# Gated delta attention with a mixture of experts: unnormalised queries, one joint sum of squares, reordered engine lists

## The reference, cut to what matters

```
q = silu(short_conv(hn @ Wq));  k = silu(short_conv(hn @ Wk));  v = silu(short_conv(hn @ Wv))
q = q * rsqrt(sum(q*q) + 1e-6) * 128 ** -0.5
k = k * rsqrt(sum(k*k) + 1e-6)
S = S * exp(g);  S = S + k (beta * (v - k.S))^T;  o = q.S            # one step per token
y = o * silu(gate);  y = y * rsqrt(mean(y*y) + 1e-5) * norm_w;  out = y @ Wo
```

## Time and profile before

| what | value |
|---|---|
| median of 3 runs | 5584.86 us (5580.64 to 5585.17) |
| the profiled execution | 5584.48 us, span 5582.7 us |
| busy over the span | PE 5247.8 us (94%), DVE 4446.0 (80%), ACT 3294.2 (59%), POOL 2364.0 (42%) |
| stretch 0 to 280 us (layer norm, decays) | PE 146.51 us, DVE 190.45, granted TensorE clock 0.79 |
| stretch 280 to 4730 us (the units) | PE 4297.46, DVE 4126.70, ACT 3113.79, POOL 2305.09, clock 1.00 |
| stretch 4730 to 5583 us (output projection and mixture) | PE 803.78, DVE 128.90, ACT 82.97, POOL 0.00, clock 0.97 |

### The profile page before, as it was taken

How to read it: one execution, slowest core, us unless ns; L and a number is a source line. 1 busy time by engine, 2 the same in 40 slices (tenths; PEclk the granted TensorE clock), 3 DMA queues, 4 the chain that set the end, 5 groups by cost and what they waited for, 6 DMA issues and landing times. The chain is left out here.

```text
span 5582.7 us, 88628 instructions
## 1 busy us (share of the span) xinstructions
PE 5247.8 (94%) x27460; PEld 3612.7 (65%) x27460; DVE 4446.0 (80%) x8285; ACT 3294.2 (59%) x6732; POOL 2364.0 (42%) x3687
## 2 busy tenths in 40 slices
PE   5599999999999999999999999999999998899999
PEld 2277777777777777777777777777777776344444
DVE  6699999999999999999999999999999997121110
ACT  3377767676767676767776767676767675010110
POOL 2155555555555555555555555555555553000000
PEclk8799999999999999999999999999999999899999
DMA  2111111111111111111111111111111110331121
GB/s 79 42 33 39 31 38 31 38 32 38 32 37 32 38 32 38 32 38 32 39 32 37 33 38 32 37 32 38 32 37 33 30 32 19 117 106 62 64 77 51
DMA packets 192055, 235.77 MB, mean 42 GB/s; under 512 B 41576, under 2 KB 136424, under 8 KB 187504
## 3 DMA queue, kind: packets, MB, share of 16 engines
q1 hardware_dynamic: 111016, 188.22, 11.5%
q10 hardware_dynamic: 80584, 41.95, 2.6%
HBM read 183.75 MB, written 46.38 MB: 41 GB/s over the span
## 5 line engine op out<-in xcount | busy, mean ns | idle before, releaser
L739 PE MATMUL bank<-xT,weights 128*128 128x512 f32 x4096 | 2090.9, 608 | 33.2 <-PEq L157 33.2
L1060 DVE SCALAR_TENSOR_TENSOR conv<-pre,taps,conv 128x512 f32<-128x512 f32 x1152 | 1006.4, 882 | 13.3 <-ACT conv L1284 8.1
L758 PE MATMUL bank<-KQ,KR 128*128 128x128 f32 x7168 | 984.5, 280 | 8.0 <-DVE KQ L1075 7.2
L758 PEld LDWEIGHTS bank<-KQ,KR 128*128 128x128 f32 x7168 | 895.9, 191 | 84.1 <-issue 61.5
L1075 DVE TENSOR_TENSOR KQ<-KQ,decay_u 128x512 f32<-128x512 f32 x896 | 868.9, 970 | 56.9 <-PE bank L758 40.3
L739 PEld LDWEIGHTS bank<-xT,weights 128*128 128x128 f32 x4096 | 675.6, 192 | 297.0 <-issue 286.0
L1507 POOL TENSOR_TENSOR KR<-KR,decay_u 128x256 f32<-128x256 f32 x768 | 579.9, 755 | 537.8 <-PE bank L758 537.1
L1090 DVE COPY_PREDICATED all_pairs<-level_mask,bank 128x512 f32<-128x512 int32 x896 | 794.1, 886 | 0.0
L1364 ACT ACTIVATE X<-bank 128x256 fp32r<-128x256 f32 x768 | 296.8, 386 | 601.4 <-PE bank L816 601.4
L1501 POOL TENSOR_TENSOR KR<-KR,decay_u 128x128 f32<-128x128 f32 x128 | 117.1, 915 | 1187.3 <-PE bank L758 1187.3
L790 PEld LDWEIGHTS bank<-T_inv,pairs 128*128 128x128 f32 x1536 | 275.5, 190 | 318.0 <-issue 303.2
(11 more groups left out here) (192 smaller groups left out, 9568.0 us busy)
## 6 DMA issues: line engine op xcount, KB each, us to landing
decay_u<-decay_scratch SPq DMA_DIRECT2D x128, 510.0 KB
beta_u<-beta_scratch SPq DMA_DIRECT2D x128, 256.0 KB
y_in<-y_scratch SPq DMA_DIRECT2D x32, 1024.0 KB, 4.8
y_scratch<-y_rn ACTq DMA_DIRECT2D x112, 256.0 KB, 2.3
xt<-in_L_attn_hidden_states SPq DMA_DIRECT2D x8, 1024.0 KB, 5.4
x_in<-in_L_attn_hidden_states SPq DMA_DIRECT2D x28, 256.0 KB, 5.1
out<-o_out ACTq DMA_DIRECT2D x28, 256.0 KB, 2.0
w<-in_L_ffn_W SPq DMA_DIRECT2D x8, 704.0 KB, 5.0
```

Of the source, the lines that this page charges most:

```text
L739: last = nc.tensor.matmul(bank[w % 2][:], weights[par][:, w, k, :], xT[:, k, u % J * UC:(u % J + 1) * UC], start=k == 0, stop=k == KC - 1)
L758: last = nc.tensor.matmul(to[:, :, i], KR[:, cols(i)], halves(KQ[:, :, cols(i)], l, 1), start=True, stop=True)
L1060: nc.vector.scalar_tensor_tensor(conv[:, w], taps_from(w, t), taps[par][:, w, t:t + 1], conv[:, w], ALU.mult, ALU.add).then_inc(steps.sem, 1)
```

## The change

1. The queries stay unnormalised. ScalarE writes SiLU of the convolved queries straight into KQ and squares them with a factor into `out_sq[a % 4]`; the query's norm, its square's rest on GpSimd, its sum on TensorE, Ln and Exp on ScalarE and the scaling on VectorE (L1195) are gone.
2. GpSimd adds the squares of the gated output to `out_sq` (`add_squares`), ScalarE rounds the total to float32r (`round_squares`), GpSimd takes what the rounding lost (`out_squares_left`), and TensorE sums both with a float32r matrix of 1/128 in place of the float32 product. The epsilon of the last root becomes 1e-5·1e-6·128.
3. KQ is doubled (`KQ[a % 2]`): the unit's inputs wait for `scan_ready` of unit b, not of m.
4. The halo of queries and keys is two copies of 16 elements.
5. The lists are reordered: level 0 ahead of one projection piece on TensorE; on VectorE the three query taps in a row at the start, the halo of queries and keys directly after the last identity, ahead of the first value tap and the scaling of level 5, and the residual ahead of the hats; on ScalarE the table load behind `take_delta`, and `round_squares` ahead of `take_right_side`; on GpSimd `first_x` behind the key scaling of level 4, followed by `add_squares`.
6. The last token's query goes the same way as the others: its own sum, norm and scaling are gone, and its squares are added to the last sum as a second matmul. The setup has one more memset and one more copy for the new constants.

Not shown in the diff are the declarations of the tiles and semaphores, and the renamed indices that follow from them.

```diff
-            def sums(which):
+            def key_sums():
 
                 if a is None:
                     return
-                wait(pe, squares_rest_ready, a, which + 1)
-                if which == 1:
-                    wait(pe, sums_taken, a, 1)
-                elif m is not None:
-                    wait(pe, sums_taken, m, 2)
+                wait(pe, squares_rest_ready, a, 1)
+                if m is not None:
+                    wait(pe, sums_taken, m, 1)
                     if c is not None and c >= 1:
                         pe.wait_ge(y_sums_free, c)
-                nc.tensor.matmul(bank[2][:], ones_r[:], squares[:, which, :], start=True, stop=False)
-                nc.tensor.matmul(bank[2][:], ones_r[:], squares_rest[:, which, :], start=False,
+                nc.tensor.matmul(bank[2][:], ones_r[:], squares[:], start=True, stop=False)
+                nc.tensor.matmul(bank[2][:], ones_r[:], squares_rest[:], start=False,
                                  stop=True).then_inc(sums_done.sem, 1)
...
-                    wait(pe, sums_taken, a, 2)
-                wait(pe, y_sq_ready, c, 1)
-                if m == LAST_UNIT:
-                    pe.wait_ge(tail_q_steps, 3)
-                nc.tensor.matmul(bank[2][:], mean_ones[:], y_sq[:], start=True, stop=True).then_inc(y_sums_done.sem, 1)
+                    wait(pe, sums_taken, a, 1)
+                wait(pe, out_sq_rest_ready, c, 1)
+                nc.tensor.matmul(bank[2][:], mean_r[:], out_sq_r[:], start=True, stop=False)
+                nc.tensor.matmul(bank[2][:], mean_r[:], out_sq_rest[:], start=False,
+                                 stop=True).then_inc(y_sums_done.sem, 1)
...
             project(2, (0, 1))
             inverse_z(1)
+            level(0)
             project(2, (2,))
-            level(0)
             inverse_t(1)
...
             first_delta()
-            sums(0)
             level(6)
             refine(b, 0)
-            sums(1)
-            if m == LAST_UNIT:
-                tail_sum()
+            key_sums()
             project(1, (0, 1))
             transpose_keys()
             y_sums()
...
-                if first:
-                    nc.vector.memset(pre[:, rows, :, 0:TAPS], 0.0).then_inc(ready.sem, 1)
-                else:
-                    nc.vector.tensor_copy(pre[:, rows, :, 0:TAPS], pre[:, rows, :, P:P + TAPS]).then_inc(ready.sem, 1)
+                for w in rows:
+                    if first:
+                        last = nc.vector.memset(pre[:, w, :, 0:TAPS], 0.0)
+                    else:
+                        last = nc.vector.tensor_copy(pre[:, w, :, 0:TAPS], pre[:, w, :, P:P + TAPS])
+                last.then_inc(ready.sem, 1)
...
-                wait(dve, rnorm_ready, a, 2)
-                nc.vector.tensor_tensor(k_hat, silu[:, 1], rnorm[:, 1], ALU.mult).then_inc(hats_ready.sem, 1)
+                wait(dve, rnorm_ready, a, 1)
+                nc.vector.tensor_tensor(k_hat[:], k_hat[:], rnorm[:], ALU.mult).then_inc(hats_ready.sem, 1)
...
-                if m is not None:
-                    wait(dve, scan_ready, m, 1)
-                decay = products(s.odd, 0)
-                nc.vector.scalar_tensor_tensor(KQ[:, 0], k_hat, -1.0, decay, ALU.mult, ALU.mult)
-                nc.vector.scalar_tensor_tensor(KQ[:, 1], silu[:, 0], SCALE, rnorm[:, 0], ALU.mult,
+                if b is not None:
+                    wait(dve, scan_ready, b, 1)
+                wait(dve, q_sq_ready, a, 1)
+                nc.vector.scalar_tensor_tensor(KQ[a % 2][:, 0], k_hat[:], -1.0, products(s.odd, 0), ALU.mult,
                                                ALU.mult).then_inc(unit_ready.sem, 1)
 
             place_last_query()
...
             place_last_query()
-            convolve(0, (1,))
-            halo(m, s.m_first, b, v_conv_steps, TAPS - 1, slice(2, 3), v_halo_ready)
+            convolve(0, (1, 2, 3))
+            halo(m, s.m_first, b, v_conv_steps, TAPS - 1, (2,), v_halo_ready)
             normalised_output()
             correct_delta(0)
             add_identity_to_z(1)
-            convolve(0, (2,))
             scale(0)
             keep_pairs(0)
             take_residual(c, 1)
...
             scale(2)
             keep_pairs(2)
             gated_output()
-            convolve(0, (3,))
             convolve(1, (1,))
             add_identity_to_z(4)
             scale(3)
...
             convolve(1, (2, 3))
             add_identity_to_z(5)
             scale(4)
-            convolve(2, (1,))
             keep_pairs(4)
             add_identity_to_z(6)
+            last_query()
+            halo(z, s.z_first, a, qk_conv_steps, 2 * (TAPS - 1), (0, 1), qk_halo_ready)
+            convolve(2, (1,))
+            scale(5)
             convolve(2, (2,))
-            scale(5)
-            last_query()
-            halo(z, s.z_first, a, qk_conv_steps, 2 * (TAPS - 1), slice(0, 2), qk_halo_ready)
             keep_pairs(5)
             convolve(2, (3,))
             scale(6)
             keep_pairs(6)
+            take_residual(b, 0)
             hats()
-            take_residual(b, 0)
             keep_chunk_decay()
-            if m == LAST_UNIT:
-                dve.wait_ge(tail_q_steps, 4)
-                nc.vector.scalar_tensor_tensor(tail_hat[:], tail_q[:], SCALE, tail_rnorm[:], ALU.mult,
-                                               ALU.mult).then_inc(tail_hat_ready, 1)
             unit_inputs()
...
-            def silu_squares(w):
+            def silu_queries():
                 if a is None:
                     return
-                wait(act, qk_conv_steps, a, (w + 1) * (TAPS - 1))
-                if w == 0 and m is not None:
+                wait(act, qk_conv_steps, a, TAPS - 1)
+                if b is not None:
+                    wait(act, scan_ready, b, 1)
+                nc.scalar.activation(KQ[a % 2][:, 1], conv[:, 0].rearrange("p b t -> p (b t)"),
+                                     ACT.Silu).then_inc(q_silu_ready.sem, 1)
+                wait(act, q_silu_ready, a, 1)
+                nc.scalar.activation(out_sq[a % 4][:], KQ[a % 2][:, 1], ACT.Square,
+                                     scale=LN_EPS ** 0.5 / SCALE ** 2).then_inc(q_sq_ready.sem, 1)
+
+            def silu_keys():
+                if a is None:
+                    return
+                wait(act, qk_conv_steps, a, 2 * (TAPS - 1))
+                if m is not None:
                     wait(act, unit_ready, m, 1)
-                nc.scalar.activation(silu[:, w], conv[:, w].rearrange("p b t -> p (b t)"),
+                nc.scalar.activation(k_hat[:], conv[:, 1].rearrange("p b t -> p (b t)"),
                                      ACT.Silu).then_inc(silu_ready.sem, 1)
-                wait(act, silu_ready, a, w + 1)
-                nc.scalar.activation(squares[:, w], silu[:, w], ACT.Square).then_inc(squares_ready.sem, 1)
+                wait(act, silu_ready, a, 1)
+                nc.scalar.activation(squares[:], k_hat[:], ACT.Square).then_inc(squares_ready.sem, 1)
...
+            def round_squares():
+                if c is None:
+                    return
+                wait(act, out_sq_added, c, 1)
+                nc.scalar.activation(out_sq_r[:], out_sq[c % 4][:], ACT.Copy).then_inc(out_sq_rounded.sem, 1)
...
-            silu_squares(0)
+            silu_queries()
             if m == LAST_UNIT:
                 tail_squares()
             take_x(4)
...
             square_output()
             keep_z(5)
             silu_gate()
-            silu_squares(1)
+            silu_keys()
             take_t(b, 5)
             take_x(5)
+            round_squares()
             take_right_side()
             take_x(6)
-            nc.scalar.preload_act_table_set("natural_log_exp_and_others")
             take_projection(0)
             take_delta()
-            inverse_norm(0)
+            nc.scalar.preload_act_table_set("natural_log_exp_and_others")
             first_tap(0)
-            inverse_norm(1)
-            if m == LAST_UNIT:
-                tail_inverse_norm()
+            inverse_norm()
             keep_scaled()
...
+        def add_squares(u):
+
+            if u is None:
+                return
+            wait_apart(pool, y_sq_ready.sem, y_sq_ready.at(u, 1), pool_waits_passed)
+            nc.gpsimd.tensor_tensor(out_sq[u % 4][:], out_sq[u % 4][:], y_sq[:], ALU.add).then_inc(out_sq_added.sem, 1)
+
+        def out_squares_left(u):
+
+            if u is None:
+                return
+            wait_apart(pool, out_sq_rounded.sem, out_sq_rounded.at(u, 1), pool_waits_passed)
+            nc.gpsimd.tensor_tensor(out_sq_rest[:], out_sq[u % 4][:], out_sq_r[:],
+                                    ALU.subtract).then_inc(out_sq_rest_ready.sem, 1)
 
...
-                squares_left(s.a, 0)
-                squares_left(s.a, 1)
+                squares_left(s.a)
                 for l in range(2, LEVELS - 1):
                     gather_x(s.b, l, None)
```

(29 more changed lines are left out.)

85 lines of the change are left out of this document (41 added, 44 removed).

## The result

The changed kernel takes 5452.14 us (5451.18 to 5453.22, 4 runs) against 5585.01 for the kernel before; the ratio is 0.9764, with a 95% interval of 0.9748 to 0.9779. So it is 133 us faster, where 183 were forecast; the time lies in the range of 5,345 to 5,510 us. It does not lie in the forecast's own band (5,340 to 5,430, chance 0.60) but in that of the tail rival (5,430 to 5,530, chance 0.27).

What follows compares the result with a forecast made beforehand. TensorE was taken as the bound, VectorE close behind. Per step 34.94 − 0.86 − 0.51 − 0.40 + 0.35 = 33.5 us, for the run −183 us to 5,401; own band 5,340 to 5,430 (0.60), range 5,345 to 5,510.

Steps and rivals of the forecast that it cites:

- tail rival: Step's end: ScalarE's T of level 0 late for the first inverse product, 0.70 us a step; 5,430 to 5,530 us, chance 0.27.
- TensorE's own work: Query sum gone (0.52 us) and output sum as two float32r matmuls (0.34 saved): 0.86 us a step, 110 us.
- The wait on delta: TensorE's level-pair product waits for ScalarE's delta; moving table load and halo copies gains 67 of 83.7 us, 0.13 a step stays.
- XX: TensorE's inverse product waits for GpSimd's XX, 0.40 us a step; moving the third query tap removes all 51 us.
- The pair of casts: GpSimd's small casts, 1.36 us beside two VectorE taps; one tap moved away saves 0.47 us.
- The new wait: Rounding on ScalarE waits for GpSimd's addition, delaying X for TensorE's first delta: 0.35 us a step, 45 us lost.
- slower rival: Between last identity and scaling of level 5, two halo copies each wait out a GpSimd instruction: 5,663 us, chance 0.07.
- level 6 on VectorE: Sign of the late step end: TensorE waits at level 6 on VectorE.
- T of level 0 late on ScalarE: Before the first inverse product: 0.67 us of slack becomes a 0.70 us wait unless ScalarE's chain starts earlier.

Runs made afterwards that it cites:

- experiment 1: The changed kernel with the first value tap put back between VectorE's scaling of level 4 and the pairs of level 4: 5335.10 us.
- experiment 5: The changed kernel with GpSimd's product and subtraction for the key squares cut to 16 of 512 columns, a probe only: 5302.44 us.
- experiment 2: The changed kernel with the halo of queries and keys as one copy of 32 elements again, in its new place: 5450.26 us.
- experiment 3: The kernel before with only the lists reordered, both norms, the float32 product and the single pair buffer kept: 5538.50 us.
- experiment 8: The changed kernel with the first value tap put back, and last query and halo copies also ahead of the last identity: 5353.22 us.
- experiment 9: The changed kernel with the first value tap put back, and the last query's instructions moved behind the new state: 5325.58 us.
- experiment 10: The changed kernel with the first value tap put back, and the last query's instructions behind the three query taps: 5320.23 us.

## Why the prediction was right, and what was off

The direction and the range were right, and so were the causes of what goes: TensorE's work and the two waits. That the time lies in the range is in part luck: the wait that was priced did not come, two others did, together three times as large, and larger gains than forecast paid for some of it.

**TensorE's own work: right.** Forecast 0.86 us a step, measured 0.52 for the query sum and 0.31 for the output sum. Another 0.09 us goes in the transpose ahead of the output sum (L932 to L943 0.44 us, L930 to L939 0.35), 0.92 in all.

**The wait on delta: right in cause, too small in size.** The halo and the table load held ScalarE, and with both moved the wait is gone. Forecast were 0.51 us. Start to start, level 6 to the refinement became 1.69 − 0.99 = 0.70 us shorter, and the refinement to the key sum another 0.07 (0.89 to 0.82). The forecast had taken the reported idle time of 0.64, which leaves out what the modelled end of the group ahead covers, and had kept 0.13 of it. The same holds for XX: 0.40 forecast, 1.50 − 1.02 = 0.48 measured. The pair of casts took 0.88 us in place of 1.36, as forecast for one tap less beside them.

**The new wait: the wrong place.** This is the step that failed. The chain of first X, addition, rounding and right side was given a slack of 0.1 us and priced at 0.35. In the changed kernel GpSimd's scaling, first X and addition took 3.59 us from start to end (1169.34 to 1172.93), not 3.80, ScalarE's part behind them 1.89 instead of 2.06, and the chain began 0.2 us earlier in the step. ScalarE had X at 1174.85 and TensorE needed it at 1175.50: 0.65 us of slack.

```profile
1174.46 0.39 ACT L1363 ACTIVATE X<-bank 128x256 fp32r<-128x256 f32 x1
```

Over the whole run this wait is 3.5 us, where 45 were forecast. The wait came at level 6, where the working of the slower rival had left 0.15 us to spare. It had taken the tap at its free length of 0.74 and the scaling at its mean of 0.97, and had neither of them wait out a whole GpSimd instruction, though the rows had shown a tap at 1.52 us; they took 1.53 and 1.76. From the identity's start to the scaling's end 2.82 us were forecast and 3.86 measured. The price was 0.82 us. A second wait that had no term in the sum is the refinement at the start of the step on VectorE's correction of delta: from the step's first instruction to the end of that part (L816 and L821, the first product with ZI) it is 5.88 us, where it was 5.59. Per step: 34.94 − 0.92 − 0.77 − 0.48 + 0.82 + 0.29 = 33.88, as measured. Experiments 1 and 5, which take the two blocks away in different ways, both come to 32.79 us, shorter by the 0.82 and by the 0.28 at the start of the step.

**The tail of the step (0.27): the nearest of the rivals.** The time lies in its band. It named "level 6 on VectorE" as one of its two signs and 5,446 us for half of its price. Its own mechanism, T of level 0 late on ScalarE, did not decide: T was ready at 1151.52 and used at 1151.61, so 0.09 us of the 0.67 was left, about the time of a handover.

```profile
1151.14 0.38 ACT L1355 ACTIVATE T_inv<-bank 128x256 fp32r<-128x256 f32 x1
```

**The slower rival: excluded.** The two halo copies cost 0.38 us together, and one copy in their place changes nothing (experiment 2). The rule of the Trainium skill (VectorE: DVE Perf Modes, Mode 2×_2P), by which both shapes take both ports, was not wrong (in experiment 3 a copy in this place waited, 1.04 us), but the first copy met only the last of a short key scaling, which ended at 1173.51, and the second followed it at once and met nothing of its own.

**What the forecast missed as a gain.** It took the list for given and asked only what it would cost. The 1.89 us of idle time in front of a queue that is late afterwards was there to be found by the same placing: the identity waits for TensorE's sixth product, which does not come earlier because VectorE has nothing to do.

## What to carry to other kernels

When two engines are both busy for over 90% of a step, the saved work of one is worth only as much as the other's next deadline allows: here some 108 us of TensorE's work brought 47 in the old order and 86 in the new one (133 − 47). Place the new lists against each other by start times, and look for an engine that idles just ahead of its own deadline; moving one instruction into that gap was worth 117 us, nearly as much as the whole change. And put small VectorE instructions where GpSimd is idle, since beside it each may cost a whole GpSimd instruction (1.18 us for four elements in experiment 8). Last, count a step on the engine that bounds the kernel: the long step was 34.57 us on VectorE and 33.91 on TensorE, and only the latter gave the gains of experiments 9 and 10.

## What the runs showed of the hardware

- In the changed kernel a VectorE instruction with two inputs in SBUF that started while a GpSimd instruction ran ended 0.55 us after it, at two to two and a half times its free length (1.53 and 1.76 us against 0.74 and 0.70). Two in a row were blocked by two GpSimd instructions in a row, one each. Two halo copies in a row passed together (0.38 us). The Trainium skill (SBUF — State Buffer, Who interferes with whom) gives the exclusive lock, and the runs agree with it.
- The contention needs no size: instructions with two inputs and 4 elements a partition took 0.58 us on average in experiment 1's place, where GpSimd works, and 0.22 in experiment 10's.
- A float32r matmul pair on 512 columns took 0.52 to 0.55 us start to start, a float32 product of the same size 0.86.
- The idle time reported ahead of a matmul group is short of the loss from start to start by about 0.2 us: for the wait on delta before, 0.64 reported against 1.69 − 0.86 = 0.83, where 0.86 is what level 4 takes up to the next group without a wait. The ends of matmuls are modelled.
